# A graph kernel: two intermediate tensors kept in SBUF, target scores loaded by period, and a deeper row buffer between the layers

## What is computed

```python
xn = layernorm(x)
# graph attention, twice: 8 heads of 64, then 1 head of 256
feat = h @ W;  el, er = (feat*attn_l).sum(-1), (feat*attn_r).sum(-1)     # per head
e    = leaky_relu(el[src] + er[dst], 0.2)
ex   = exp(e - segment_max(e, dst)[dst])
out  = segment_sum(ex/segment_sum(ex, dst)[dst] * feat[src], dst)        # elu between the two
# linear attention over all nodes, 8 heads of 32
q, k = elu(xn @ Wq)+1, elu(xn @ Wk)+1;  context = k.T @ v;  mix = (q @ context)/(q @ k.sum) @ Wproj + bproj
x = x + gat2(elu(gat1(xn))) + mix
x = x + moe(layernorm(x))                                                # 8 dense experts of 3 layers, gated
```

## Time and profile before

| | |
|---|---|
| median of three runs | 3706.5 us (3697.7 to 3708.5) |
| profiled execution, its own time | 3723.8 us |
| span of the profile | 3722.0 us |
| busy in the span | DVE 67%, POOL 59%, PE 59%, ACT 52% |
| stages in the span | node pass to 180 us, index pass to 326, first edge pass to 1742, hidden pass to 2056, second edge pass to 3722 |
| mean granted clock of TensorE | 0.739 |

### The profile page before, as it was taken

The page is one execution under the profiler, slowest core; times in us unless marked ns, Lnnn a source line. Parts: engine busy times, 40 slices in busy tenths (PEclk is TensorE's granted clock), DMA queues, the critical chain, the costliest instruction groups (busy, mean ns, idle before and its releaser), DMA issues. The chain is left out here.

```text
span 3722.0 us, 35760 instructions
## 1 busy us (share of the span) xinstructions
PE 2183.5 (59%) x7456; PEld 1368.4 (37%) x7456; DVE 2507.0 (67%) x6180; ACT 1933.9 (52%) x6365; POOL 2196.7 (59%) x2113
## 2 busy tenths in 40 slices
PE   5800355545544455443555001787888888888999
PEld 4600233323332333222444001454555444454565
DVE  5882798989988888887666234555666565655742
ACT  2400787878766676664344122444555444454642
POOL 2336676667766676663565666666766666666400
PEclk8955676766655555555788555889999989998999
DMA  8713899999999999996443456555555555555510
GB/s 235 197 20 93 308 372 357 358 357 373 374 334 363 363 362 365 358 367 239 110 114 90 119 178 206 155 171 173 188 182 168 156 172 174 184 172 172 165 53 10
DMA packets 282617, 828.81 MB, mean 223 GB/s; under 512 B 72960, under 2 KB 150896, under 8 KB 260863
## 3 DMA queue, kind: packets, MB, share of 16 engines
q0 software_dynamic: 129184, 385.13, 34.0%
q1 hardware_dynamic: 122270, 420.46, 29.4%
q10 hardware_dynamic: 30944, 20.94, 2.1%
HBM read 432.76 MB, written 394.56 MB: 222 GB/s over the span
## 5 line engine op out<-in xcount | busy, mean ns | idle before, releaser
L1363 POOL DMA_INDIRECT e_rows<-scratch_table,k_src x1680 | 1769.6, 1053 | 874.1 <-issue 414.1
L1479 ACT ACTIVATE e_rows<-e_rows,e_wr 128x64 f32<-128x64 f32 (+1 forms) x4200 | 1215.4, 371 | 35.8 <-issue 26.8
L1456 DVE SCALAR_TENSOR_TENSOR e_ring<-e_ring,e_kext,e_rows 128x512 f32<-128x512 f32 (+1 forms) x1568 | 965.1, 616 | 391.0 <-ACT e_rows L1479 183.6
L2115 PE MATMUL e_p_y<-e_wfo,e_h 128*112 128x256 f32 x1792 | 435.0, 397 | 132.8 <-DVE e_y L1877 122.5
L2115 PEld LDWEIGHTS e_p_y<-e_wfo,e_h 128*112 128x112 f32 x1792 | 328.2, 185 | 251.8 <-issue 122.2
L2089 PE MATMUL e_p_a<-e_xt,e_wf 128*128 128x448 f32 x896 | 375.3, 562 | 26.1 <-ACT e_h L2024 14.1
L1877 DVE SCALAR_TENSOR_TENSOR e_y<-e_p_y,e_w,e_y 112x256 f32<-112x256 f32 x448 | 194.6, 476 | 289.5 <-remote 183.5
L2024 ACT ACTIVATE e_h<-e_p_a,e_shift,e_scale 128x448 f32<-128x448 f32 x224 | 156.5, 720 | 445.6 <-remote 280.9
L2101 PE MATMUL e_p_b<-e_h,e_wf 128*128 128x448 f32 x896 | 363.9, 549 | 15.1 <-issue 8.1
L1012 PE MATMUL e_p_c<-e_vext,e_kphi 112*128 112x129 f32 x224 | 67.4, 454 | 335.0 <-DVE e_kphi L902 170.6
L2024 ACT ACTIVATE e_h<-e_p_b,e_shift,e_scale 128x448 f32<-128x448 f32 x224 | 157.0, 720 | 177.1 <-remote 91.1
(11 more groups left out here) (406 smaller groups left out, 3581.7 us busy)
## 6 DMA issues: line engine op xcount, KB each, us to landing
scratch_sums<-e_ring SPq DMA_DIRECT2D x56, 2112.0 KB
scratch_sums<-e_ring SPq DMA_DIRECT2D x56, 1848.0 KB
scratch_sums<-e_ring SPq DMA_DIRECT2D x56, 1032.0 KB
scratch_sums<-e_ring SPq DMA_DIRECT2D x56, 903.0 KB
e_rows<-scratch_table,k_src POOLq DMA_INDIRECT x1680
scratch_table<-na_frow ACTq DMA_DIRECT2D x56, 227.5 KB
scratch_table<-hi_frow ACTq DMA_DIRECT2D x56, 115.5 KB
na_x<-in_x SPq DMA_DIRECT2D x7, 896.0 KB, 18.5
```

Source lines behind the costliest of these rows:

```text
L1363: nc.gpsimd.indirect_dma_start(out=rows[:, n % B, g, :], out_offset=None, in_=table, in_offset=bass.IndirectOffsetOnAxis(ap=k.src[:, n * G ...
L1456: nc.vector.scalar_tensor_tensor(ring[:, i, j - c0, 0:W], prev, kext[:, 0, j + 1:j + 2], rows[:, rb, j, 0:W], ALU.mult, ALU.add).then_inc( ...
L1479: last = nc.scalar.activation(rows[:, rb, j, at], rows[:, rb, j, at], ACT.Copy, scale=wr[:, b, h, j + 1:j + 2])
L2115: last = nc.tensor.matmul(self.p_y[bank][0:BK, i * D:(i + 1) * D], self.h2[:, e % 2, kt, v:v + BK], self.wfo[:, e, kt, :], start=kt == 0, ...
```

## The change

Three edits. **First**, `k.feat`, a tensor of 128 by 56 by 2 by 112 fp32, holds the turned rows of all tiles in SBUF: ACT writes it in the node pass, PE reads it, and `Mixing` overwrites each tile's part with the queries once it is projected. The stores and loads of `turned` and `queries` go, with their waits (ACT's before line 349 and DVE's before the queries among them), and `exps`, `att`, `none` share other tiles. **Second**, `er` holds two periods of 60 columns; SP loads a period one tile after the one before it began, POOL gathers the first targets' scores of period 0 before the rows and the other 13 between the row gathers of tile B (2 in the first pass, 3 in the second), and DVE copies and scans the next period's scores between the steps of tile 2 of each period. **Third**, the hidden pass has 12 row buffers, and the scatter is that of tile n-12.

```diff
@@ node_pass, SP and ACT
-            for n in range(NB):
-                sp.wait_ge(xt_ready, n + 1)
-                sp.dma_start(k.turned[:, n * 2 * BK:(n + 1) * 2 * BK], xt[:, n % 2, :, :].rearrange("p m v -> p (m v)")
-                             ).then_inc(xt_out[n % 2], 16)
...
                 act.wait_ge(t_ready, n + 1)
-                wait(act, f_ready, n - 1)
-                wait(act, xt_out[b], n // 2 * 16)
-                nc.scalar.copy(xt[:, b, :, :], p_t[b][:, 0:2 * BK].rearrange("p (m v) -> p m v", m=2)).then_inc(xt_ready, 1)
+                nc.scalar.copy(k.feat[:, n, :, :], p_t[b][:, 0:2 * BK].rearrange("p (m v) -> p m v", m=2)).then_inc(xt_ready, 1)
@@ Mixing
-            sp.wait_ge(self.q_kept, t + 1)
-            sp.dma_start(self.k.queries[:, t * 2 * BK:(t + 1) * 2 * BK], self.qt[:, :]).then_inc(self.q_out, 16)
-            if t + 2 < NB:
-                self.load_turned(sp, t + 2)
...
-        wait(dve, self.q_out, t * 16)
-        nc.vector.scalar_tensor_tensor(self.qt[:, :], self.p_q[:, 0:2 * BK], 0.0, self.exps[:, D:D + 2 * BK],
+        nc.vector.scalar_tensor_tensor(k.feat[:, t, :, :].rearrange("p m v -> p (m v)"), self.p_q[:, 0:2 * BK], 0.0, self.low[:, D:D + 2 * BK],
@@ edge_pass, SP, POOL and DVE
+            def er_load(q):
+                wait(sp, d_ready, PB * (q - 1))
+                sp.dma_start(er[:, q % 2, :, :].rearrange("p j h -> p (j h)"), starts_by_lane[:, q, :]).then_inc(er_in[q % 2], 16)
...
+                if n % PB == 1 and 2 <= n // PB + 1 < Q:
+                    er_load(n // PB + 1)
...
+            first_er(0)
             for n in range(NB):
                 for g in range(G):
+                    if n == B and 1 <= g < Q:
+                        first_er(g)
                     wait(pool, summed, (n - B) * G + g + 1)
...
+            def er_along(n, j):
+                q = n // PB + 1
+                if n % PB != PB - 2 or q >= Q:
+                    return
+                if j == 1:
+                    er_first(q)
+                if 1 <= j < 1 + H:
+                    er_scan(q, j - 1)
@@ hidden_pass
+    HB = 3 * KB
-        rows = s.sb("rows", [BK, 2 * KB, 2, L.row])
+        rows = s.sb("rows", [BK, HB, 2, L.row])
...
-                wait(pool, agg_ready, n - 2 * KB + 1)
+                wait(pool, agg_ready, n - HB + 1)
...
-                if n >= 2 * KB:
-                    scatter(n - 2 * KB)
+                if n >= HB:
+                    scatter(n - HB)
```

More of the change, by code:

```diff
@@ L850, in sync_first, with load_input @@
         sp.dma_start(self.bproj[:, :], a["bproj"]).then_inc(self.loaded, 16)
-        for t in (0, 1):
-            self.load_turned(sp, t)
-    def load_turned(self, sp, t):
-        wait(sp, self.projected, t - 1)
-        sp.dma_start(self.xt[:, t % 2, :, :].rearrange("p m v -> p (m v)"),
-                     self.k.turned[:, t * 2 * BK:(t + 1) * 2 * BK]).then_inc(self.xt_in[t % 2], 16)
-    def load_query(self, sp, t):
-        wait(sp, self.ad_ready, t - 1)
-        sp.dma_start(self.q[:, t % 2, :], self.k.queries[:, t * 2 * BK:(t + 1) * 2 * BK]).then_inc(self.q_in[t % 2], 16)
+    def load_input(self, sp, t):
         wait(sp, self.res_ready, t - 1)
@@ L1207, in vector_join @@
         c.base, c.n = q * 6, 1
-        wait(dve, self.out, 16 * (2 * q + 2) if q else 0)
+        dve.wait_ge(self.out, 16 * (2 * q + 2))
         c(nc.vector.tensor_tensor(self.tl[:, 0:W].rearrange("p (h e) -> p h e", h=H),
@@ L1551, in _ @@
                                                  ).then_inc(rows_in[b], 16)
-                if n >= 2 * KB:
-                    scatter(n - 2 * KB)
-            for n in range(NB - 2 * KB, NB):
+                if n >= HB:
+                    scatter(n - HB)
+            for n in range(NB - HB, NB):
                 scatter(n)
@@ L2204, in gps_kernel @@
     with Scope(nc, "k") as k:
-        k.turned = scratch("turned", (P, NB * 2 * BK))
-        k.queries = scratch("queries", (P, NB * 2 * BK))
         k.dst_pad = scratch("dst_pad", ((Q + 2) * CAP,), I32)
```

99 lines of the change are left out of this document (49 added, 50 removed).

## The result

The changed kernel takes 3667.9 us (median of four, 3664.8 to 3669.7), the kernel before 3702.1 on the same chip (3696.2 to 3708.5): ratio 0.991, interval 0.9895 to 0.9926. It is faster by 34 us where 94 were forecast, and lies above the range (3568 to 3650).

A forecast was written before the change was run, and what follows sets the result against it. It took DVE, with DMA close behind, to bound the first edge pass, and PE to lead the second. Node pass -18, first edge pass -3, hidden pass -57 and second edge pass -16 made -94, scaled to 3613 us; range 3568 to 3650.

The forecast's parts named there:

- Start of the first edge pass: First edge pass: one score gather instead of 14 ahead of the rows brings head 0 20.6 us sooner; -18 us counted.
- second edge pass: Second edge pass: rows start sooner behind one score gather, tiles 0 to 2 come 16.4 us sooner; -16 us counted.
- head starts are lost: Rival, chance 0.19: node pass wins only 10, head 2 waits in the first edge pass, second pass's -16 is lost; 3642 us.
- 4 us to spare: Second edge pass: the 13 moved scores land at 2156.4 us, and DVE needs them at 2160.4.
- Hidden pass: Pass between the layers: twelve row buffers end POOL's score waits, groups go from 21.05 to 17.0 us; -57 us.
- POOL becomes the bound: Hidden pass: POOL's twelve issues, taken as 17.0 us a group, set the pace, against DVE's need of 15.0.
- the waits of 78.1 us end: Hidden pass: with scatters twelve tiles behind, POOL no longer waits for ACT's scores, 78.1 us before.
- Node pass: Node pass: ACT's wait of 24.5 us for a turned tile's store goes, row stores are late next; -18 us.
- assumed slow store: Node pass: if a row store took 8 us, two buffers allow a tile per 4 us, and 14 us are won.
- Scores along the way: First edge pass: DVE copies and scans scores in each of 13 later periods; +18 us, bounds +10 and +30.
- Less DMA: First edge pass: 19.3 MB of turned and query traffic gone, a quarter of DVE's DMA waits saved; -3 us.
- bytes bind: Rival, chance 0.12: the first edge pass goes at the pace of its bytes, 53 us won there instead of 3; 3563 us.

The follow-up runs named there:

- f2_pause_tiles: Changed kernel, in both edge passes POOL waits before each tile's gathers, from the second tile on, until the previous tile's rows landed: 3858.2 us, ratio 1.0405.
- e3_no_hidden12: Changed kernel with the pass between the layers put back to eight row tiles, so the first two edits alone: 3691.8 us, ratio 0.9965 to the kernel before.
- e2_scores: Kernel before with only the second edit, target scores period by period: 3706.4 us, ratio 1.0001.
- e4_er0_ahead: Changed kernel with all fourteen gathers of first scores ahead of the row gathers again in both edge passes: 3660.0 us, ratio 0.9881 to the kernel before.
- r3_er0_ahead: Changed kernel with all gathers of first scores ahead of the rows, in a later comparison (kernel before 3710.6 us): 3677.7 us, ratio 0.9904.
- r4_idle48: Changed kernel with 48 one-element DVE fills before head 0 of the second edge pass, kernel before at 3710.6 us: 3682.2 us, ratio 0.9922.
- e7_idle48: Changed kernel with 48 one-element DVE fills before head 0 of the second edge pass, kernel before at 3504.9 us: 3430.2 us, ratio 0.9794.

## Why the prediction was wrong

*Start of the first edge pass (-18), second edge pass (-16).* These steps failed. Head 0 moved as worked out (22.8 us after the first score gather; forecast about 23), but the step "tiles 0 to 2 come 16.4 us sooner, and PE, which is the bound later, starts its experts sooner by as much" took the tiles behind head 0 to follow their rows. At the level of 3705 us they do not: in the changed kernel the last gather for tile 4 of the second pass is issued by 2117, and head 4 comes at 2146 without waiting for rows. DVE and ACT go at a slow pace of their own there, and head 4 lies 139 to 143 us behind the start of the first pass (without pauses of POOL) and about 147 behind that of the second, whatever is done for head 0: in fourteen traces at this level (all but that of `f2_pause_tiles`) the second pass has it at 143.6 to 153.4 us with head 0 at 26.3 to 69.9. The trace of before showed the pace. In the earlier trace rows the step at 2176.76 belongs to a stretch of such steps, and I read its place only to see whether scores would be late. "Less if the first tiles are slow" was as near as the forecast came.

A second fault is in the same step. For the first pass the sum counts what the thirteen moved gathers do to the rows behind them (16.3 us of POOL, up to 6 given back). For the second it asks only when their scores land and puts the delay of tile 3's rows at nothing, though it is the same 16.3 us. At the level of 3705 us the slow pace hides that, at 3505 us it is what shows. The rival "head starts are lost" had the right price for the second start (16) and a third of that for the first (5, where 18 went). Its causes, late scores and row stores, were not what took the starts back in the changed kernel's trace; but the 4 us to spare for the scores hold only as long as DVE is slow.

*Hidden pass (-57).* Right in kind, too large: -34 in the profiles, -33 with the edit alone. By size this term, 23 us too large, is the largest miss of the sum. The failed step is "POOL becomes the bound" with "the waits of 78.1 us end". They fell from 78 to 46 us. The forecast has the last group's shares 219.5 us after the first gather (1743 to 1962.5); with the first group's shares 13 us after it, as measured, that is 15.9 us a group, 13 times. Measured are 17.6, which is 22 us more. Of the 17.6 us some 13 are DVE's work (forecast 15.0) and 4.5 are waits, half of them by name for ACT. The runs at the level of 3505 us have 15.8 us a group with the same hidden pass.

*Node pass (-18).* -12.9, and 12.7 between `e3_no_hidden12` and `e2_scores`. The mechanism was the one named, the row stores behind full DMA; ACT waited 19.6 us for them, and the gain is near that of the assumed slow store (-14). No run shows the 8 us assumed for a store; the longest wait was 6.4 us.

*Scores along the way (+18).* +7. A scan took 0.28 us as forecast, but of the 23 us of work most fills gaps: in the first half only the first of the later periods is longer (94 against 92 us), in the second most by 1 us. The bounds (+10, +30) did not reach low enough.

*Less DMA (-3), and the rival "bytes bind".* 0. The Trainium skill (SBUF — State Buffer, the section on a bandwidth-pool intuition) would have the stage follow its bytes; with 19.3 MB less it stayed within 0.1 us, so the trace does not agree here. Of the forecast's -3 nothing came.

Sums do not close fully: the edits apart give -33, 0 and -15, the whole -33 (0.991 and 0.9914). The changed kernel was not in the comparison of the edits; `e4_er0_ahead`, which was, has -45, nearly the sum. The intervals are 5 to 7 us each way, and head 4 to the end of the second pass varies from 1503 to 1537 us over the traces at this level (`f2_pause_tiles` left out). Whether 15 us are lost between the edits stays open.

What is shown: a head start is worth nothing by head 4 at the level of 3705 us (`e4_er0_ahead`, `r3_er0_ahead`); DVE stands between instructions that wait for nothing (the fills), at one level and hardly at the other; and pauses of POOL move the slow stretch (three of them keep it out of tiles 0 and 1). What is only argued: that it is the instructions that come late, that POOL's gathers have to do with it, and that the same stretches the groups between the layers and the 104 us a period of the second pass where the other level has 90. What stays open: why there are two levels, and what holds the instructions up; the packets of the instruction queue do not tell.

## What to carry to other kernels

Before a sooner start is counted as won, look at the pace of the next tiles: instructions of 0.1 to 0.5 us at even distances of 0.7 or 1.4 us, with "issue" or a semaphore long done as the reason, are a sign that the engine goes at a pace that neither data nor its own work sets, and work done sooner only waits there. The start of a pass, with POOL's gathers in a long unbroken run, is where this case had it. Count, too, what a moved instruction delays at its new place. And have the kernel before measured beside the changed one each time: the change was worth 0.9% at one level and, with small additions, 2.1% at the other.

## What the runs showed of the hardware

At the level of 3705 us DVE got most of 41 fills of 0.06 us 1.40 us apart (2024.7 to 2071.0 in `r4_idle48`), with a DMA share of 0.4 and no packet on the instruction queue up to 2064; at the level of 3505 us 48 fills took 1.12 us. The Trainium skill (Runtime: NRT & Kernel Launch, the section on instruction fetch mechanics) says that each sequencer fetches its next 16 KiB of instructions by its own DMA queue while it runs the present ones, and that the cost of crossing from one such block to the next is mostly hidden. The trace shows instruction queues and their packets (1.28 MB in 156 on q14), at either level. Whether the slow stretch is such a fetch that is not hidden no run here shows. By head 4 the level of 3705 us is 16 to 18 us behind the other in the first edge pass and 26 in the second (146.2 against 120.7).

Both levels run the first edge pass from head 8 on at the same pace: 92.0 to 92.5 us a period in its first half, 97 to 99 in its second, 102 in the one between. Of the 240 us between the spans of the changed kernel (3664.7) and of `e7_idle48` (3425.1), 16 lie between head 0 and head 4 of the first pass, 24 between the layers, and nearly all the rest in the second pass, with periods of 104 and 90 us.
